# A pre-norm attention and expert layer on one core: products with V of two groups in one PSUM bank, one transpose of a group's maxima, W1 staged where W2 is, and another order of the work

## What is computed

```python
def _L0_attn_ref(x, w_qkv, b_qkv, w_proj, b_proj):      # x: (8, 512, 128), 16 heads of 8
    qkv = x @ w_qkv + b_qkv
    ...
    attn = jnp.einsum('bhqd,bhkd->bhqk', q, k) * scale
    attn = jnp.where(causal, attn, -jnp.inf)
    attn = jax.nn.softmax(attn, axis=-1)
    out = jnp.einsum('bhqk,bhkd->bhqd', attn, v)
    ...
    return out @ w_proj + b_proj
def _L0_ffn_ref(x, Wg, bg, W1, b1, W2, b2):              # 8 experts, hidden width 512
    probs = jax.nn.sigmoid(x_flat @ Wg + bg)
    weights = probs * (probs > 0.5)
    h = jax.nn.relu(jnp.einsum('td,edh->eth', x_flat, W1) + b1[:, None, :])
    expert_out = jnp.einsum('eth,ehd->etd', h, W2) + b2[:, None, :]
    return jnp.einsum('te,etd->td', weights, expert_out)
x = x + attn(layernorm(x))
x = x + ffn(layernorm(x))
```

## Time and profile before

| | us |
|---|---|
| median of three runs | 724.9 (723.68 to 725.62) |
| the profiled execution | 725.9 |
| its span, first to last instruction | 724.2 |
| PE busy | 674.6 (93%) |
| DVE, ACT, POOL busy | 462.4, 453.2, 371.5 |
| mean granted TensorE clock | 0.966 |

### The profile page before, as it was taken

The page is one execution under the profiler, slowest core; times in us unless marked ns, Lnnn a source line. Parts: engine busy times, 40 slices in busy tenths (PEclk is TensorE's granted clock), DMA queues, the critical chain, the costliest instruction groups (busy, mean ns, idle before and its releaser), DMA issues.

```text
span 724.2 us, 13238 instructions
## 1 busy us (share of the span) xinstructions
PE 674.6 (93%) x4515; PEld 456.9 (63%) x4515; DVE 462.4 (64%) x933; ACT 453.2 (63%) x841; POOL 371.5 (51%) x441
## 2 busy tenths in 40 slices
PE   3858787999999999999999999999999999999995
PEld 2423354666766676667666776667666766678774
DVE  7983657766865588656865686667766576435332
ACT  2453555766766776666766686667767666666552
POOL 5261123445645575555555566456455545556564
PEclk9966889999999999999999999999999999999998
DMA  6701113212121103221221113110221101001110
GB/s 185 206 14 36 25 25 83 66 41 54 39 83 55 53 16 92 67 52 32 70 68 54 39 37 100 54 54 2 69 68 53 39 32 46 31 30 46 58 30 14
DMA packets 28673, 40.23 MB, mean 56 GB/s; under 512 B 3936, under 2 KB 12648, under 8 KB 28608
## 3 DMA queue, kind: packets, MB, share of 16 engines
q1 hardware_dynamic: 28080, 39.20, 19.4%
q10 hardware_dynamic: 528, 0.20, 0.1%
HBM read 23.52 MB, written 2.23 MB: 36 GB/s over the span
## 4 chain that ended last, share of the span: by engine, by line
PE 81%; DVE 9%; issue 4%; POOL 3%; SPq 1%; ACT 1%; DMA 0%; POOLq 0%; DVEq 0%; ACTq 0%
PE ring L1163 10%; PE y_bank L1207 9%; PE ring L1090 9%; PE ring L1031 8%; PE ring L1033 8%; PE ring L1032 8%; PE y_bank L1211 8%; PE y_bank L1209 8%; PE ring L1102 5%; PE ring L1037 4%; PE ring L1152 2%; DVE xn L841 2%; DVE pm L944 2%; DVE negmax L944 1%; PE y_bank L1163 1%
## 5 line engine op out<-in xcount | busy, mean ns | idle before, releaser
L695 POOL TENSOR_TENSOR h_lo<-h_all,h_hi 128x512 fp32r<-128x512 f32 x128 | 164.6, 1286 | 153.2 <-ACT h_all L803 148.4
L797 ACT ACTIVATE h_hi<-ring 128x512 fp32r<-128x512 f32 x256 | 153.6, 600 | 114.9 <-PE ring L1033 83.9
L764 ACT ACTIVATE pt<-ring 128x512 f32<-128x512 f32 x315 | 176.1, 600 | 33.3 <-PE ring L1090 31.4
L944 DVE TENSOR_REDUCE negmax<-ring 128x1 f32<-128x512 f32 (+1 forms) x189 | 123.6, 683 | 62.7 <-PE ring L1102 62.0
L688 POOL TENSOR_SCALAR_AFFINE_SELECT pt<-pt 128x512 f32<-128x512 f32 x128 | 79.8, 637 | 115.3 <-ACT pt L764 115.2
L994 DVE SCALAR_TENSOR_TENSOR h_lo<-ring,h_hi 128x512 fp32r<-128x512 f32 x128 | 87.7, 685 | 59.7 <-ACT h_hi L797 59.6
L1207 PE MATMUL y_bank<-h_hi,w_lo 128*128 128x512 f32 x256 | 112.5, 440 | 3.5 <-DVE f_buf L1007 1.7
L1031 PE MATMUL ring<-x2T_lo,w_hi 128*128 128x512 f32 x256 | 108.3, 423 | 0.0
L1090 PE MATMUL ring<-stack 32*128 32x512 f32 (+3 forms) x1005 | 93.6, 371 | 13.2 <-DMA stack<-nmT 2.6
L1033 PE MATMUL ring<-x2T_hi,w_hi 128*128 128x512 f32 x256 | 101.1, 395 | 0.0
L1032 PE MATMUL ring<-x2T_hi,w_lo 128*128 128x512 f32 x256 | 101.1, 395 | 0.0
(11 more groups left out here) (130 smaller groups left out, 828.3 us busy)
## 6 DMA issues: line engine op xcount, KB each, us to landing
f_buf<-gates SPq DMA_DIRECT2D x64, 256.0 KB, 3.3
stack<-parts SPq DMA_DIRECT2D x96, 128.0 KB
x_in<-in_L_attn_x SPq DMA_DIRECT2D x8, 256.0 KB, 2.8
pt<-in_L_ffn_W SPq DMA_DIRECT2D x1, 2048.0 KB, 10.0
out_x<-f_buf SPq DMA_DIRECT2D x8, 256.0 KB, 2.2
stack<-stack SPq DMA_DIRECT2D x32, 16.0 KB
stack<-nmT SPq DMA_DIRECT2D x32, 16.0 KB
wqkv_in<-in_L_attn_w_qkv ACTq DMA_DIRECT2D x1, 192.0 KB, 2.7
```

What stands on the lines that cost most here:

```text
L695: g_.tensor_tensor(h_lo[:, (i * SLOTS + s) % 3, :], h_all[:], h_hi[:, (i * SLOTS + s) % 3, :].bitcast(F32), ALU.subtract).then_inc(s_hlo_p ...
L764: sc.activation(pt[:, slot, :], b[:], ACT.Exp, scale=SCALE).then_inc(free_sem("ex", i, g, u), 1)
L797: sc.activation(h_hi[:, (i * SLOTS + s) % 3, :], bank_of("z", i, s)[:], ACT.Relu).then_inc(s_hhi, 1)
L944: v.tensor_reduce(dst, src, AX.X, ALU.max, negate=True).then_inc(free_sem("max", i, g, u), 1)
```

## The change

1. **Two groups' products with V share a bank.** In `v_sb` the odd groups' heads have their 9 columns behind those of the even groups (`v_of`), so that `pv` of groups 0 and 1 (2 and 3) add up in one bank and fill rows 0 to 8 and 9 to 17 of each 32. The odd `pv` takes the bank of the even one. `og`, `oT` and the division on DVE are done once for two groups: 16 of each in place of 32. Exponentials that reuse a slot wait for `s_pv_even` where the group is even.
2. **One matmul transposes the maxima of a group**: `nm` is 128 x 128 in place of 128 x 4 x 128, the result 32 x 128 in place of 8 x 512, and `mrow` is two DMAs.
3. **W1 lands in `f_buf`**, like W2; W2's load waits for PE's last use of W1. Exponentials no longer wait for `w1`.
4. **POOL_SPLITS** leaves out slots 7, 15, 23 and 31: 12 of 32 slots on POOL, 20 on DVE.
5. **Order.** In the first 50 units exponentials come 18 units behind maxima (with visits of exponentials alone to catch up), W1's and W2's items are due later, `SWITCH_DUE` and `PV_DUE` are 1.5 and 2, costs are others, engines' overlaps are modelled, and a table `SHIFT` moves due times by item. `k` comes before `q`, and the preparation of b1 comes behind both.

```diff
-POOL_SPLITS = [s for s in range(SLOTS) if s % 2 == 1]
+POOL_SPLITS = [s for s in range(SLOTS) if s % 2 == 1 and s % 8 != 7]
...
-FFN_LAG = 55
+HEAD_LAG, HEAD_UNITS = 18, 50
+FFN_LAG = 54
...
-SWITCH_DUE = 0.3
-PV_DUE = 0.3
+SWITCH_DUE = 1.5
+PV_DUE = 2
...
+SHIFT = {('act', 'exp', False): 2,
...
+         ('pe', 'nm', False): -35.5,
...
+    for k in range(0, len(units) + EXP_LAG, 2):
+        lag = HEAD_LAG if k <= HEAD_UNITS else EXP_LAG
...
-    put("sp", ("w2load", None), -8.9, 600, ("sp", ("stack", 0, 0)))
+    put("sp", ("w2load", None), -8.9, 600, ("pe", ("w1", EXPERTS - 1)))
...
-                put("act", ("exp", i, g, u), at + .3, 600, ("pe", ("ex", i, g, u)),
-                    ("pe", ("w1", EXPERTS - 1)))
+                put("act", ("exp", i, g, u), at + .3, 600, ("pe", ("ex", i, g, u)))
...
     def fill(item):
+        if item[0] == "pv" and item[2] % 2:
+            use[item] = use[(*item[:2], item[2] - 1)]
+            return
...
-        w1_in, w2_in = pt[:, PT_SLOTS - EXPERTS:, :], f_buf
+        w1_in = w2_in = f_buf
...
                 elif kind == "w2load":
+                    sp.wait_ge(*full("w1", EXPERTS - 1))
...
-                    sp.dma_start(rows[M_ROW::M_STEP, :, 0, :],
-                                 nmT[:, g % 2, :].bitcast(F32)).then_inc(s_mrow[g], 16)
+                    for n in range(2):
+                        sp.dma_start(rows[M_ROW::M_STEP, n, 0, :],
+                                     nmT[16 * n:16 * n + 16, g % 2, :].bitcast(F32)
+                                     ).then_inc(s_mrow[g], 16)
...
-                    for t in range(TB):
-                        last = mm(b[:, t * P:(t + 1) * P], nm[:, t, :], ident32[:], start=True, stop=True)
-                    last.then_inc(done, 1)
+                    mm(b[:, 0:P], nm[:], ident32[:], start=True, stop=True).then_inc(done, 1)
...
-                                      start=(kb == 0), stop=(kb == TB - 1), skip_group_check=True)
-                    last.then_inc(done, 1)
+                                      start=(kb == 0 and g % 2 == 0),
+                                      stop=(kb == TB - 1 and g % 2 == 1), skip_group_check=True)
+                    last.then_inc(done if g % 2 else s_pv_even, 1)
```

More of the change, by code:

```diff
@@ L88, in put @@
         if (engine, item[0]) in latest and item[0] not in ("max", "ex"):
-            before.append((engine, latest[(engine, item[0])]))
+            before.append(("turn", (engine, latest[(engine, item[0])])))
         latest[(engine, item[0])] = item
+        due += SHIFT.get((engine, item[0], item[1] == 0), 0)
         work[(engine, item)] = (due, cost, before)
@@ L244, in list_schedule @@
     for key, (_, _, before) in work.items():
-        before = {b for b in before if b in work}
+        before = {b for b in before if b in work or b[0] == "turn"}
         missing[key] = len(before)
@@ L286, in start @@
         idle[engine] = False
-        at(now + cost, "idle", engine)
+        at(now + cost - OVERLAP.get(engine, 0), "idle", engine)
+        at(now + cost - OVERLAP.get(engine, 0), "turn", key)
         late = {"pe": AFTER_PE, "sp": AFTER_DMA}.get(engine, AFTER_OTHERS)
@@ L319, in pick_pe @@
             if item[0] == "pv":
-                if free and (pv is None or due < pv[0]):
+                if (free or item[2] % 2) and (pv is None or due < pv[0]):
                     pv = (due, key)
@@ L339, in pick_pe @@
                 if best is None or due < best[0]:
-                    if pv and form == "full" and free > len(mx) + len(ex):
+                    if pv and form == "full" and free + item_odd(pv) > len(mx) + len(ex):
                         start(now, "pe", pv[1])
@@ L366, in list_schedule @@
                 continue
-            if key in emptier:
+            if what == "done" and key in emptier:
                 holder[emptier[key]] = None
-            for other in opens.get(key, ()):
+            for other in opens.get(("turn", key) if what == "turn" else key, ()):
                 missing[other] -= 1
@@ L490, in block_program @@
         s_xTact = sem("s_xTact")
[L491 removed]
+        s_qkhi = [sem(f"s_qkhi{n}") for n in range(2)]
         s_stack = [sem(f"s_stack{g}") for g in range(GROUPS)]
@@ L865, in _ @@
                     dve.wait_ge(s_vset, 1)
-                    v.memset(v_sb[:, :, :, HD:HD + 1], 1.0).then_inc(s_vset, 1)
+                    for o in range(2):
+                        v.memset(v_of[:, :, o, :, (HD + 1) * o + HD:(HD + 1) * (o + 1)],
+                                 1.0).then_inc(s_vset, 1)
                 elif kind == "b1":
```

182 lines of the change are left out of this document (111 added, 71 removed).

## The result

The changed kernel took 690.4 us, median of 4 runs (689.2 to 691.5), beside 724.9 us: a ratio of 0.9526, 95% interval 0.9505 to 0.9547. The forecast was 686 us with a range of 677 to 704. The profiled execution took 690.3 us, with a span of 688.5.

What follows compares the result with a forecast made beforehand. PE was taken to bound the body and the end, a chain of waits the stretch to the first `y`. 725.9 − 20.5 (head) − 18.1 (body) − 2.8 (end) + 2.0 (bank) = 686.5, forecast 686 us, range 677 to 704.

Steps and rivals of the forecast that it cites:

- The head: Stretch up to the first `y`: DVE's work plus idle time at `pv` and visits puts it at 102 us, 20.5 earlier.
- Rival 1: Before the first `y`: clock stays low, `pv` takes 4.3 us and stops DVE longer; 700 us in total, chance 0.16.
- its sign of being wrong: Forecast counts as wrong if the first `y` moves by less than 10 us or periods exceed 79 us.
- nm: PE's transposes of maxima in the body: three of four matmuls go at 0.098 us each, 26 groups, 7.7 us gained.
- oT: PE's transposes in the body: 13 of 16 removed steps lie behind the first `y`, 0.44 us each, 5.7 us gained.
- Form changes: PE in the body: 15 fewer entries from full into scores, 10 fewer exits from pv into full, 2.4 us gained.
- The bank: Body: an even `pv` holds one of seven banks until the odd `og`, so visits may lack one; 2.0 us added.
- not under 5: Sign for the body: PE would wait less than 5 us between 140 and 600 us.
- The end: Last stretch: last `y` no longer waits for a POOL split, and `term` is covered; 2.8 us gained together.
- The middle period: One period of a sequence in the body: 77.9 to 78.3 us in place of 80.3.
- Rival 5: Slower than before: visits and `z` wait for each other's banks; at 0.35 us a visit 730 us, chance 0.04.

Runs made afterwards that it cites:

- the last experiment: Changed kernel plus constant matmuls filling PE's early idle gaps (17 before the first visit) and slot 27's POOL low part moved, except in the first sequence: 678.7 us, ratio 0.9357.

## Why the prediction was right or wrong

**The head** is the step that failed: 20.5 us forecast, 10.8 found. Its first terms held. The first maximum started at 24.70 us (24.8 forecast), the early norms took 1.57 and 1.10 us (1.43), and DVE worked 65.85 us from there to the first `y` (66). What failed is the idle time added to it: 1.5 us at each of five `pv` and 3.3 us more, 10.8 in all, against 21.0. The sum priced `pv` at 2.3 us, that is with the full clock, and left the half clock to a rival. DVE and PE in the head of the changed kernel:

```profile
75.71 0.69 DVE L1005 TENSOR_REDUCE negmax<-ring 128x1 f32<-128x512 f32 x1 [4.58 <-PE ring L1165]
...
87.17 1.29 DVE L1005 TENSOR_REDUCE negmax<-ring 128x1 f32<-128x512 f32 x2 [2.40 <-PE ring L1165]
...
93.60 0.69 DVE L1005 TENSOR_REDUCE pm<-ring 128x4 f32<-128x512 f32 x1 [3.23 <-PE ring L1165]
```

```profile
69.83 4.50 PE L1226 MATMUL ring<-pt,v_sb 128*32 128x512 f32 x32
...
86.11 0.80 PE L1153 MATMUL ring<-stack 32*128 32x512 f32 x4 [1.07 <-ACT pt L818]
...
89.18 3.73 PE L1226 MATMUL ring<-pt,v_sb 128*32 128x512 f32 x32
```

Three of the five `pv` took 4.50, 3.73 and 2.90 us (before, all five took 4.05 to 4.50). DVE's waits of 4.58 and 3.23 us stand behind the two longest; that of 2.40 us stands behind a visit that waited for ACT and then ran at half clock. The runs put a size on it. With the clock up throughout the head (the last experiment), first `y` 103.9 us, DVE's idle time 13.0: so the step was about 1.9 us off in its mechanism and 7.6 us in the clock, by one execution of each. The rows of before had shown 0.77 of the clock in this stretch. In the new order PE idled only 11.1 of its 86.8 us (24.5 of 97.2 before), but it waited 5.64 us for the stacked rows ahead of the first visit, then in many small pieces for maxima, ACT and a norm, and the clock rose no higher than 0.81. Rival 1 described the head nearly as it came out, 111.5 us for its "over 112", though not the total. The head moved 10.8 us, just beyond the 10 that the prediction had set as its sign of being wrong.

**`nm`**: 10.0 us for 7.7. The mechanism was right and the term too small: the price per matmul is 0.11, not 0.098, the one that stays costs only 0.06 and not the forecast 0.10, and 1.3 us came from other places, as shown above.

**`oT`**: 6.0 us for 5.7, right.

**Form changes and short waits** are the other wrong size: 2.4 us were priced, `y` and `z` got 11.2 shorter. Sorted by what stands beside each distance, form changes give 2.6 us of it, as priced, and one `z` 0.7. Short waits that have gone give 2.7, and what the table leaves of longer waits in these rows, about 0.9. The largest part, about 4 us, is none of these: in mid-step a matmul starts 0.233 us behind the one before it throughout the kernel before, and 0.228 us throughout the changed one. With the order rules of before it is 0.230 and with a bank for each `pv` 0.233, so it goes with the program and not with the execution, but no run shows the cause. The prediction priced neither this nor the short waits. It read PE's share of busy time, 497.4 of 500 us, as no slack; a wait of 0.05 us between matmuls that overlap counts as busy there.

**The bank**: 2.0 us forecast. No visit in the body waited for `og`. (The prediction wrote that no row of before shows PE waiting for `og`; in the head of before `oT` did, 2.4 us in three places, but for its data and not for a bank.) Three visits waited 0.57 us for the bank of `q`, 1.7 us in all. The cause of these waits and of the longer ones was named only for the head: DVE's norm beside POOL's low part. The prediction followed it through two early norms, where it did no harm, and not through the body, where the new order put both norms of a sequence on it: 1.28 us in each of four periods and 0.57 in three of them. The new due times are only part of the reason, since with the order rules of before the first norm of a sequence met POOL too (0.93 us of waiting in each of four periods). So PE's waits from 140 to 600 us were 7.7 us (460 less 452.29), not under 5. DVE's work in the period was 58.7 us in place of 56.5 for the same reason.

What the Trainium skill says on it (SBUF — State Buffer, SBUF: two separate sides), that the one waits until the other's instruction ends, agrees with these rows for POOL's subtractions: 2.17 us beside one of 1.29, where 1.10 is the norm's own (81.43 us). (The norm of 2.47 us had a mask behind the subtraction.) For POOL's mask it doesn't: beside one of 0.72 us the norm takes 1.43, only 0.3 more. Its advice to rotate banks (Perfetto Trace Analysis, Matmuls), weighed in the prediction against the shared bank, was not borne out as a gain: with a bank for each `pv` a middle period waits 0.9 us less, but is 0.4 us longer, and the kernel 8.8 us slower.

**The end**: 2.8 us forecast. The last `y` started 0.26 us later than in an unbroken row, where it had been 1.34, and waits for `term` fell from 1.7 us to 0.5, as said; putting the splits back made the last `y` wait the 1.1 us again.

**The middle period** of 77.9 to 78.3 us came out at 78.27, but as 3.5 us less work and 1.5 us more waiting, not as the priced 2.45 and nothing.

**Rival 5** needed a bank less to come true. Its time (736.5 us) came at six banks and not at seven, and there its waits are only part of the cost.

## What to carry to other kernels

Where PE waits often, price its steps at the clock that the page shows there, and ask first what would fill the gaps: some 45 matmuls of constants, written into a bank that the next step has already been given, were worth 6 us. When instructions are moved, list for DVE's operations that read and write SBUF which POOL subtraction will stand beside them. And a PE that is 99% busy can still hide a few microseconds in short waits, and can run at a slightly slower pace throughout: compare the distances between starts with the shortest one, and their usual value between kernels.

## What was unexpected in the hardware

- A DVE layer norm on SBUF of four instructions takes 1.1 us alone, 1.43 beside a POOL mask of 0.72, 2.2 beside a POOL subtraction of 1.3 us (2.5 with a mask behind it), and 3.90 where it met three POOL instructions of 1.3. DVE mostly was the one that lost time, also when its first instruction had started 0.55 us ahead (330.58 against 331.13): POOL got in between DVE's instructions and took its usual 1.29 us. In the run with the moved low part POOL lost instead: its subtraction started 0.9 us into the norm at 327.81 us and took 1.38 us, and the norm its 1.11.
- The clock in the head fell to half not only behind long idle times. One fall, at 85.2 us of the changed kernel, came when PE had been busy 5.80 us of the stretch from 78.4 us on, no wait in it over 0.42; a wait of 1.07 us had begun only 0.2 us before. With fillers in the gaps before and after it, it didn't come.
- One wait of 3.25 us in the body brought half the clock for 3.4 us with it, so it cost about half as much again (an estimate).
- Taking one of seven banks away, with the order planned anew but its shifts kept, cost 45 us, more than the whole change had gained.
- A matmul of 512 columns in mid-step started 0.228 us behind the one before it in the changed kernel and in six of its variants, 0.230 with the order rules of before, and 0.233 in the kernel before and with a bank for each `pv`. The value holds from the first period to the last of each trace. Over some thousand matmuls that is 4 us, and its cause is open.
